# Low-rank products merged into the base weights once per batch, and the fillers of the attention steps put in a new order

## What is computed

```python
hidden_i = jnp.einsum('bsd,fd->bsf', x, wi)
hidden_i += ALPHA * jnp.einsum('bsr,fr->bsf', jnp.einsum('bsd,rd->bsr', x, common_wi_a), common_wi_b)
hidden_i += _expert_lora(x, expert_ids, experts_wi_a, experts_wi_b)
hidden_i = jax.nn.relu(hidden_i)
hidden_o = jnp.einsum('bsf,df->bsd', hidden_i, wo)
hidden_o += ALPHA * jnp.einsum('bsr,dr->bsd', jnp.einsum('bsf,rf->bsr', hidden_i, common_wo_a), common_wo_b)
hidden_o += _expert_lora(hidden_i, expert_ids, experts_wo_a, experts_wo_b)
```

## Time and profile before

| | us |
|---|---|
| median of 3 runs | 1477.07 |
| lowest, highest | 1468.75, 1480.15 |
| the profiled execution | 1473.53 |
| its span (first to last instruction) | 1471.8 |
| PE busy in the span | 1299.8 (88%) |
| DVE, ACT, POOL busy | 814.7, 682.5, 515.0 |

### The profile page before, as it was taken

How to read it: one execution, slowest core, us unless ns; L and a number is a source line. 1 busy time by engine, 2 the same in 40 slices (tenths; PEclk the granted TensorE clock), 3 DMA queues, 4 the chain that set the end, 5 groups by cost and what they waited for, 6 DMA issues and landing times.

```text
span 1471.8 us, 26713 instructions
## 1 busy us (share of the span) xinstructions
PE 1299.8 (88%) x8313; PEld 974.7 (66%) x8314; DVE 814.7 (55%) x1753; ACT 682.5 (46%) x1301; POOL 515.0 (35%) x809
## 2 busy tenths in 40 slices
PE   5878989988988988989989885459899999999997
PEld 3436656656656656656666554448788888888886
DVE  4626646646646646556556433745455555555553
ACT  4654654655655655655655630023333333333332
POOL 0332332332332432432332420324354444544442
PEclk9579999999999999999999978569999999999998
DMA  5112223222232132132132223733525224242220
GB/s 176 44 48 89 83 77 116 79 85 96 80 123 87 64 122 82 65 123 87 55 113 79 80 86 129 292 137 73 217 43 155 36 43 141 52 148 38 38 43 11
DMA packets 50765, 137.54 MB, mean 93 GB/s; under 512 B 10658, under 2 KB 29730, under 8 KB 49026
## 3 DMA queue, kind: packets, MB, share of 16 engines
q0 software_dynamic: 28992, 68.35, 16.4%
q1 hardware_dynamic: 21698, 68.18, 12.8%
HBM read 86.03 MB, written 51.38 MB: 93 GB/s over the span
## 4 chain that ended last, share of the span: by engine, by line
PE 71%; DVE 11%; ACT 8%; DMA 3%; issue 3%; POOL 3%; SPq 0%; POOLq 0%; DVEq 0%; ACTq 0%
PE bank L691 65%; PE bank L973 4%; DVE nmax L1359 4%; ACT q_sb L1160 3%; ACT probs_t L1153 2%; PE bank L965 1%; DVE hid_low L1286 1%; DMA xg<-hrows,gid 1%; POOL w_rest L1617 1%; ACT ot_sb L1169 1%; DMA out<-y_sb,sid 1%; POOL wsplit L1621 1%; PE bank L893 1%; DVE mm_sb L1366 1%; ACT sums L1170 1%
## 5 line engine op out<-in xcount | busy, mean ns | idle before, releaser
L1359 DVE TENSOR_REDUCE nmax<-bank 128x1 f32<-128x512 f32 (+3 forms) x512 | 221.4, 485 | 120.7 <-PE bank L691 120.4
L1153 ACT ACTIVATE probs_t<-bank 128x512 f32<-128x512 f32 (+1 forms) x384 | 181.1, 524 | 119.8 <-PE bank L691 119.3
L1193 ACT ACTIVATE g<-z 128x512 f32<-128x512 f32 x142 | 89.8, 632 | 280.6 <-DVE z L1555 280.6
L1603 POOL TENSOR_SCALAR_AFFINE_SELECT probs_t<-probs_t 128x256 f32<-128x256 f32 x256 | 97.8, 406 | 336.3 <-ACT probs_t L1153 336.1
L691 PE MATMUL bank<-wst,g1t_high 128*128 x568 | 185.7, 408 | 0.9 <-DVE g1t_low L1543 0.9
L1665 POOL DMA_INDIRECT out<-y_sb,sid x71 | 114.4, 1611 | 152.1 <-DVE y_sb L1576 69.0
L1617 POOL TENSOR_TENSOR w_rest<-w_rest,w_high 128x512 f32<-128x512 f32 x64 | 82.0, 1282 | 173.5 <-ACT w_high L1039 173.5
L1555 DVE TENSOR_TENSOR z<-bank,b_sb 128x512 f32<-128x512 f32 x142 | 98.2, 692 | 73.3 <-PE bank L691 62.6
L691 PEld LDWEIGHTS bank<-wst,g1t_high 128*128 128x128 f32 x568 | 102.6, 191 | 20.6 <-issue 1.1
L691 PE MATMUL bank<-wst,g1t_low 128*128 x284 | 113.1, 398 | 0.0
L691 PE MATMUL bank<-wst,g2t_high 128*128 x568 | 108.4, 291 | 1.5 <-DVE g2t_low L1543 1.5
(11 more groups left out here) (223 smaller groups left out, 2879.4 us busy)
## 6 DMA issues: line engine op xcount, KB each, us to landing
wst<-wsplit SPq DMA_DIRECT2D x8, 4096.0 KB, 12.5
w_rest<-in_w_all POOLq DMA_DIRECT2D x64, 256.0 KB, 2.9
wsplit<-w_high POOLq DMA_DIRECT2D x64, 256.0 KB, 2.3
wsplit<-w_rest POOLq DMA_DIRECT2D x64, 256.0 KB, 2.5
hrows<-h_sb SPq DMA_DIRECT2D x8, 528.0 KB, 4.0
x_in<-in_xT SPq DMA_DIRECT2D x8, 512.0 KB, 3.7
wb_raw<-in_lora_wb SPq DMA_DIRECT2D x8, 512.0 KB, 3.5
x1t<-in_xT SPq DMA_DIRECT2D x8, 512.0 KB, 4.3
```

The lines of the kernel that those rows point to most:

```text
L1153: taken(nc.scalar.activation(probs_t[:, (2 * g + half) % PT_SLOTS, S * u:S * u + width], at(n, rd)[:, 0:width], ACT.Exp), n, rd)
L1193: nc.scalar.activation(g[:, :], z[:, :], ACT.Gelu).then_inc(s_g, 1)
L1359: ins = V.tensor_reduce(nmax[:, g % 2, half, i:i + 1], at(n, rd)[:, cols], AX.X, ALU.max, negate=True)
L1603: ins = nc.gpsimd.affine_select(diag, diag, [[0, 2], [1, P]], ALU.is_ge, 0.0, base=0, channel_multiplier=-1)
```

## The change

The low-rank products are no longer applied to the activations. For each batch they are multiplied out, B x A, and added to the base weights: `merge 0` to `3` make the first layer's weights (pieces of 128 x 512), `merge 4` to `7` the second's. A merge is one matmul of 512 columns, or two of 256; DVE adds 2 x the product to a piece of the base weight that a DMA has staged in `w_stage`; ACT casts the sum to the high half two steps later, DVE subtracts for the low half one step after that. So low_i, low_o and the matmuls of wb and bo in hid and h go, and 8 merges per batch come, for the batch that the turn attends to. The low-rank factors are now all stored as 128 rows, split by one cast and one `scalar_tensor_tensor` each. Their loads and splits move to other steps; the base weights are loaded again for each batch, piece by piece, each load behind the DVE add before it. The fillers are dealt out anew: h 0 to 3 fill steps 5 to 22, next, ht, gate and softmax the last nine.

```diff
-FILLERS = ([(("hid", j), k) for j in range(HID_EARLY, KF) for k in range(KD)] +
-           [(("x1", t2), 0) for t2 in range(TB // 2)] + [(("low_o", 0), piece) for piece in range(LOW_PIECES)] +
-           [(("h", t), piece) for t in range(TB) for piece in range(H_PIECES)] +
-           [(("next", 0), 0), (("next", 0), 1), (("ht", 0), 0), (("next", 1), 0), (("ht", 1), 0), (("next", 1), 1),
-            (("gate", 0), 0), (("softmax", 0), 0)])
-FILL_COUNTS = [2] * 5 + [1] * 7 + [0] + [1] * 5 + [0, 1, 0, 1, 1, 1, 0] + [2] * 5 + [0, 1, 0, 1]
-LORA_STEPS = {29: (0, 1), 30: (1, 2), 31: (2, 3), 32: (3, 4), 33: (4, 6)}
-LOW_STEPS = {30: (0, 1), 32: (1, 2), 33: (2, 4)}
+HID_STEPS = [[(("hid", j), k) for k in range(KD)] for j in range(HID_EARLY, KF)]
+H_ITEMS = [(("h", t), piece) for t in range(TB) for piece in range(H_PIECES)]
+X1_STEP = [(("x1", t2), 0) for t2 in range(TB // 2)]
+
+
+def merge(n):
+
+    return (("merge", n), 0)
+
+
+MID = ([[item] for item in H_ITEMS[:7]] + [[]] + [[item] for item in H_ITEMS[7:12]] + [[]] +
+       [[item] for item in H_ITEMS[12:]] + [[], []])
+TAIL = [[(("next", 0), 0)], [(("next", 0), 1)], [(("next", 1), 0)], [(("next", 1), 1)], [(("ht", 0), 0)], [],
+        [(("ht", 1), 0)], [(("gate", 0), 0)], [(("softmax", 0), 0)]]
+FILL = HID_STEPS + [X1_STEP] + MID + TAIL
+MERGE_STEPS = {4: 0, 7: 1, 10: 2, 14: 3, 25: 4, 27: 5, 29: 6, 31: 7}
+LORA_O_STEPS, LORA_I_STEPS, LORA_FIRST_STEPS = {9: 0, 11: 1}, {19: 0, 21: 1}, {0: 0, 2: 1}
 IN_STEPS = PAIRS // 2
 CAST_STEPS = {9: 0, 15: 1, 21: 2, 27: 3, 32: 4}
 CASTS_AFTER = {("x1t", 1): 5, ("hid", 0): 6}
...
     order += [("q", 0), ("k", 0), ("x1t", 0), ("x1t", 1), ("q", 1), ("k", 1), ("v", 0)]
-    order += quads[0] + [("low_i", 0)] + quads[1] + [("hid", 0), ("v", 1)] + quads[2] + [("hid", 1)] + quads[3]
...
         def taken(ins, name, rd):
             ins.then_inc(free[rd.plan[name][0]], 1)
 
-        def base_piece(n):
-
-            if n < BASE_PIECES // 2:
-                cols = slice(n % 2 * 512, (n % 2 + 1) * 512)
-                return wi_high[:, n // 2, cols], wi_low[:, n // 2, cols], wi_raw[:, n // 2, cols]
-            rows = slice(2 * (n - BASE_PIECES // 2), 2 * (n - BASE_PIECES // 2) + 2)
-            return tuple(w[:, rows, :].rearrange("p j d -> p (j d)") for w in (wf_high, wf_low, wf_raw))
+        def merged(n):
+
+            if n < MERGES // 2:
+                k, cols = n % KD, slice(n // KD * S, (n // KD + 1) * S)
+                return wi_high[:, k, cols], wi_low[:, k, cols], wi_raw[:, k, cols], wi_t[:, k, cols]
+            rows = slice(2 * (n - MERGES // 2), 2 * (n - MERGES // 2) + 2)
+            return (*(w[:, rows, :].rearrange("p j d -> p (j d)") for w in (wf_high, wf_low, wf_raw)), wo_t[:, rows, :])
+
+        def merges(rd, step):
+
+            return [name for name, _ in rd.fillers(step) if name[0] == "merge"] if 0 <= step < STEPS else []
+
...
+            def stage_after(rd, n):
+
+                drained(sp, ("merge", n), rd)
+                stage((n + 1) % MERGES)
...
+                            ins = mm(at_bank(quad[pair], rd)[:, :], sel_sb[rows, slot + u, :], parts[rows, c, slot + u, :],
                                      start=(u == 0), stop=(u == 1))
                             if u == 1:
                                 done(ins, quad[pair], rd)
                     return
-                elif what == "low_i":
+                elif what == "merge":
                     vacant(pe, n, rd)
-                    pe.wait_ge(s_x_low, p * KD + KD)
-                    pe.wait_ge(s_lora_low, p * LORA_LOWS + 1)
-                    for k in range(KD):
-                        for x in (x_high, x_low):
-                            ins = mm(dst()[:, :], at_cat[:, k, :, :].rearrange("p c r -> p (c r)"), x[:, k, :],
-                                     start=(k == 0 and x is x_high), stop=(k == KD - 1 and x is x_low))
-                elif what == "low_o":
-                    if piece == 0:
-                        vacant(pe, n, rd, [("hid", j) for j in range(KF)])
-                        pe.wait_ge(s_lora_low, p * LORA_LOWS + 3)
-                    per = KF // LOW_PIECES
-                    for j in range(per * piece, per * (piece + 1)):
-                        for g in (hid_high, hid_low):
-                            ins = mm(dst()[:, :], ao_cat[:, j, :, :].rearrange("p c r -> p (c r)"), g[:, j, :],
-                                     start=(j == 0 and g is hid_high), stop=(j == KF - 1 and g is hid_low))
-                    if piece < LOW_PIECES - 1:
-                        return
+                    if m == 0:
+                        pe.wait_ge(s_lora_low, LORA_PARTS * b + 2)
+                    if m == MERGES // 2:
+                        pe.wait_ge(s_lora_low, LORA_PARTS * b + 4)
+                    if m < MERGES // 2:
+                        k, cols = m % KD, slice(m // KD * S, (m // KD + 1) * S)
+                        ins = mm(dst()[:, :], at[:, k * P:(k + 1) * P], wb[:, cols], start=True, stop=True)
+                    else:
+                        for u in range(2):
+                            j = 2 * (m - MERGES // 2) + u
+                            ins = mm(dst()[:, u * D:(u + 1) * D], ao[:, j * P:(j + 1) * P], bo[:, :], start=True, stop=True)
                 elif what == "x1t":
...
-                    if m == 0:
-                        pe.wait_ge(s_lora_low, p * LORA_LOWS + 2)
+                        vacant(pe, n, rd)
+                        if m == 0:
+                            pe.wait_ge(s_x_low, p * KD + KD)
+                            pe.wait_ge(s_merge_low, p * MERGES + 2)
+                        if m == KF // 2:
+                            pe.wait_ge(s_merge_low, p * MERGES + 4)
                     for k in range(KD) if piece is None else (piece,):
                         cols = slice(m * P, (m + 1) * P)
                         for w, x in ((wi_high, x_high), (wi_high, x_low), (wi_low, x_high)):
-                            mm(dst()[:, :], w[:, k, cols], x[:, k, :], start=(k == 0 and w is wi_high and x is x_high),
-                               stop=False)
+                            ins = mm(dst()[:, :], w[:, k, cols], x[:, k, :], start=(k == 0 and w is wi_high and x is x_high),
+                                     stop=(k == KD - 1 and w is wi_low))
                     if piece not in (None, KD - 1):
                         return
-                    ins = mm(dst()[:, :], wb[:, m * P:(m + 1) * P], low_i[:, :], start=False, stop=True)
                 elif what == "h":
                     if piece == 0:
                         vacant(pe, n, rd, [("hid", j) for j in range(KF)] if m == 0 else ())
+                        if m == 0:
+                            pe.wait_ge(s_merge_low, (p + 1) * MERGES)
                     per = KF // H_PIECES
                     for j in range(per * piece, per * (piece + 1)):
                         rows = slice(m * P, (m + 1) * P)
                         for g, w in ((hid_high, wf_high), (hid_high, wf_low), (hid_low, wf_high)):
-                            mm(dst()[:, 0:D], g[:, j, rows], w[:, j, :],
-                               start=(j == 0 and g is hid_high and w is wf_high), stop=False)
...
+            def lora_high(parts_of, b, m):
+
+                raw, _, width, _ = parts_of[m]
+                n = LORA_PARTS * b + (2 if parts_of is lora_o else 0) + m
+                act.wait_ge(s_lora_o if parts_of is lora_o else s_lora_i, 32 * (b + 1))
+                if n:
+                    act.wait_ge(s_lora_low, n)
+                nc.scalar.copy(lora_top[:, 0:width], raw[:, :]).then_inc(s_lora_high, 1)
+
+            def merge_high(rd, n):
+
+                drained(act, n, rd)
+                high, _, raw, _ = merged(n[1])
+                nc.scalar.copy(high, raw).then_inc(s_merge_high, 1)
...
+            def lora_low(parts_of, b, m):
+
+                raw, split, width, mark = parts_of[m]
+                dve.wait_ge(s_lora_high, LORA_PARTS * b + (2 if parts_of is lora_o else 0) + m + 1)
+                V.scalar_tensor_tensor(split[:, :], lora_top[:, 0:width].bitcast(F32), marks_sb[:, mark:mark + 1],
+                                       raw[:, :], ALU.mult, ALU.add).then_inc(s_lora_low, 1)
+
+            def merge_low(b, n):
+
+                high, low, raw, _ = merged(n[1])
+                dve.wait_ge(s_merge_high, MERGES * b + n[1] + 1)
+                V.tensor_tensor(low, raw, high.bitcast(F32), ALU.subtract).then_inc(s_merge_low, 1)
 
             def take(rd, n, piece=None):
...
+                elif what == "merge":
+                    dve.wait_ge(s_stage, 16 * (MERGES * b + m + 1))
+                    if p is not None:
+                        filled(dve, ("hid", 3) if m < 2 else ("hid", KF - 1) if m < MERGES // 2 else ("h", TB - 1), rd)
+                    filled(dve, n, rd)
+                    ins = V.scalar_tensor_tensor(merged(m)[2], at_bank(n, rd)[:, :], 2.0, w_stage[:, :], ALU.mult, ALU.add)
```

332 lines of the change are left out of this document (141 added, 191 removed).

## The result

The changed kernel takes 1506.91 us (median, 1500.7 to 1509.1) against 1478.06 for the kernel before, measured beside it: a ratio of 1.0206 (95% interval 1.0164 to 1.0248), slower. The forecast was 1469, and its range ended at 1492. The profiled execution took 1509.1 us, its span is 1507.4, which is 35.6 more than before (the medians are 28.9 apart: of the changed kernel the profile has the slowest execution).

The account below looks back on a forecast made before the run. TensorE was taken as the bound, full in the opening and steps 5 to 18. Seven middle turns -1.5 us, last turn -8.4, batch 0 +2: -8 in all, 1469 us against 1477.1; 8-in-10 range 1438 to 1492.

Parts of the forecast that it names:

- Opening: Start of each middle turn: eight matmuls and the wait before hid 0 go, TensorE being full, -2.6 us a turn.
- last turn: Final turn, feed-forward alone: no merges, so all removed low-rank matmuls and a 1.45 us wait count, -8.4 us.
- steps 0 to 4: After the opening: four wb matmuls go, waits for VectorE grow, merge 0 is added, +0.2 us a turn.
- steps 5 to 18: Middle stretch of a turn: TensorE's own work -0.2, new bank wait +2.5, VectorE and ScalarE load +1.0 us.
- steps 19 to 24: Forecast with steps 13 on: merge 3, two bo matmuls fewer, 1.6 us more VectorE splits, +0.4 us a turn.
- steps 25 to 33: End of a middle turn: row-block pieces leave, merges come, value product starts earlier, -1.5 us a turn.
- The hand-over: Steps 5 to 18: TensorE waits twice for VectorE's copy of h in bank 7, 1.5 and 0.94 us, +2.5 a turn.
- VectorE's and ScalarE's load: Steps 5 to 12: added adds, splits and casts crowd both engines, partly absorbed, +1.0 us a turn.
- Batch 0: First batch, attention alone: eight merges at half clock, half of them in TensorE's idle end, +2 us.
- The slower one: Rival: idle ends of turns 1 to 6 drop the clock to half, 28 us more, 1497 us; chance 0.17.
- The faster rival: Bank hand-overs and crowded VectorE steps cost nothing, 3.5 us a turn fewer, 1444 us; chance 0.33.
- the port that VectorE and GpSimd share: Added low halves and splits would sometimes collide with GpSimd's subtractions, about 1 us of VectorE time a turn, within bounds.

Follow-up runs that it names:

- e10: e6 with the matmuls of merges 4 to 7 issued twice over, same result: 1441.09 us, ratio to before 0.9761.
- e11: Kernel before, only ScalarE's casts moved: piece 5 behind low_i, 6 behind hid 3, 7 in step 3; last turn's too: 1465.25 us, ratio 0.9922.
- e5: Changed kernel with ScalarE's routed-weight casts later: piece 5 behind qs 2, 6 behind hid 3, 7 in step 3; last turn's too: 1461.5 us.
- e14: e10 with the casts of routed-weight pieces 5, 6 and 7 back in the changed kernel's places: 1489.81 us, ratio to before 1.0104.
- e2: Changed kernel with h 0 to 3 in banks 7, 3, 7, 3 again and merge 2 in bank 7: 1488.64 us.
- e9: e6 with the second layer's low-rank factors split in steps 19 and 21, the next first layer's in 26 and 28: 1450.21 us.
- e13: e10 with the second layer's low-rank factors split in steps 16 and 18, the next first layer's in 21 and 23: 1442.85 us.
- e4: Changed kernel with the matmuls of merges 4 to 7 issued four times over, same result: 1511.09 us, ratio to before 1.0242.
- e6: Changed kernel with both the later casts of e5 and the h and merge banks of e2: 1448.91 us, ratio to before 0.9831.
- e3: Changed kernel with w_stage loads after the first cut to 16 columns and ao_raw loaded later, output wrong: 1510.28 us.
- e7: Kernel before without three low_i matmuls and the wb matmuls of hid 0 to 3 per opening, output wrong: 1470.96 us, ratio 0.9968.

## Why the prediction was wrong

**The step that failed** is in *Opening*: "PE is full here, so I count all of it", and "What is late next is the pair of x_low halves". I looked for the next thing among what the change touches and left out what stands in ACT's queue for the routed block. With every opening counted to the end of the wait for hid_low, as above, the forecast was -2.6 us each and -18 over the seven. Measured: -1.6 us in the best (turn 6, 25.2 for 26.8), +5.5 in the worst (turn 5, 32.1 for 26.6), +6 over the seven. With the casts moved (e10, all seven turns) it is 22.7 us. That is 3.8 below the mean of before, but there the clock stood at half as six of the seven openings began; against the one opening of e11 that ran at full clock (turn 6, 25.2) it is -2.5. So the size of the term was right, its cover was not. The same step failed in the last turn: -8.4 forecast, -2.0 measured, -8.8 with the casts moved (e5). e14 against e10 puts the price of this one thing at 49 us, e5 against the changed kernel at 45. It is larger than the whole loss.

By stretch, against the kernel before, every opening counted to the end of that wait:

| sum over seven turns, us | forecast | changed kernel | e10 |
|---|---|---|---|
| opening | -18 | +6 | -26 |
| steps 0 to 4 | +1 | 0 | -8 |
| steps 5 to 18 | +23 | +25 | +9 |
| steps 19 to 24 | +3 | +8 | +13 |
| steps 25 to 33 | -10 | -6 | -11 |
| last turn (once) | -8 | -2 | -11 |

**The hand-over** was foreseen, with its place and its mechanism: +2.5 forecast, 1.7 us of waiting a turn and 1.3 of length (e2). The first wait was sized rightly (1.5, measured 1.35 to 1.73), the second was not (0.94, measured 0.26). Mis-sized was also what it does to the clock: I had looked for falls only at the turn's end, and they came in steps 9 to 12 as well, in three of seven turns.

**VectorE's and ScalarE's load** in steps 5 to 12: +1.0 forecast, 0.9 measured (e9, e13), though the splits cost as much wherever they were put. Steps 5 to 18 together were forecast at some 34 us and took 33.9 in turn 3. Steps 19 to 24 gave +1.0, where I had let 1.6 us of splits pass for nearly nothing (+0.4, with merge 3).

**Steps 0 to 4** were forecast at +0.2. Counted from the end of the wait for hid_low they take 13.0 to 13.1 us for 13.5, -0.4, inside the bounds given; in turns 5 and 6, where the clock was at half in them, 14.6. In e10, with the cast of piece 7 out of step 1, they take 12.3. **The end of the turn**: -1.5 forecast, -1.6 measured where the clock held. **Batch 0**: +2 forecast. Turn 1 starts 1.7 us later, but that agreement is luck: the batch itself takes as long as before, with 2.2 us more of TensorE's work beside its waits, and what moved is its start, for which the forecast had nothing.

**The rivals.** The slower one had the right side, and its number (1497) came nearer than the forecast, by luck, since it looked in the wrong place: of the six ends one fell (turn 2), which is worth some 6 us, and e4, which holds the clock up at the ends, is no faster. It was right that idle time in front of TensorE is paid twice, as a wait and in the clock behind it: 92.2 us at half clock in place of 37.5 in the same turns. The Trainium skill (TensorE: Matmul & The Clock Gate, Part 1) says of waits in the middle of a kernel that the clock gate closes again and the matmuls behind them start slow; the trace agrees, and e5, which takes waits away and touches nothing else, brings the 92.2 us to 68.3. The faster rival assumed costless hand-overs; e6 and e10 reach its place (1449 and 1441) once the casts are moved too.

Of the port that VectorE and GpSimd share (the Trainium skill, SBUF — State Buffer) the prediction said that it might add 1 us a turn. The split of ao took up to 1.72 us beside POOL's masks, where that of wb, of the same shape, took 1.28 throughout, and low halves of 0.68 took up to 1.61 beside POOL's subtraction. That agrees, and it is small.

**Open.** Opening 5 is the slowest in nearly every version that keeps the casts (e3 30.7, changed kernel 32.0, e7 26.9): between POOL's two stores of piece 37 the trace has 2.61 us with no releaser, and I did not find out why. Why the load of piece 5 takes 4.3 to 5.7 us in the changed kernel is not shown either; e3 lightened the traffic and the load was still slow. And how the 49 us of the casts divide between waits and clock over the whole kernel was not separated: every run that removed a wait also removed half clock.

## What to carry to other kernels

Where an engine is busy for 97% of a stretch, as TensorE was in the opening, work taken from it pays only until something else is late: before counting it, walk through every in-order queue that feeds the stretch and ask of each instruction that waits for a DMA how much earlier it would have to be ready. A background chain with its own round trip (here 8.6 us) that is placed by hand beside the work of one version has to be placed again when that work shrinks. And judge such a change only after its neighbours have been moved, in both kernels: as it came the edit is 2.1% slower, with the casts and banks moved 1.7% faster (e6), of which 0.8% are to be had in the kernel before by the casts alone (e11); e10 reaches 2.4%, with a doubling of matmuls that was not tried on the kernel before.

## What the runs showed of the hardware

Doubling eight small matmuls in a stretch where TensorE waits made the kernel 8 us faster (e6 to e10), with time at half clock down from 47.8 to 23.9 us: redundant matmuls can pay. Fourfold issue in the changed kernel did not (e4). A wait of 1.35 us in an otherwise full stretch was followed at once by half clock for 6.8 us in turns 5 and 6 (and one of 1.73 us in turn 4), and in turns 1, 2, 3 and 7 the same wait was not. A store and a load of 256 KB, 2.8 and 2.9 us from issue at their quickest, took up to 5.2 and 5.7 us at the start of a turn in the changed kernel; in e10, where loads took as long, that cost the openings nothing.
